# The four row-group tails of a head's scores put in front of its four wide matmuls

## The reference

```python
q, k, v = (split_heads(x @ w + b) for w, b in ((wq, bq), (wk, bk), (wv, bv)))
scores = jnp.einsum('bhqd,bhkd->bhqk', q, k) * scaling + attn_bias[:, None, :, :]
attn = jax.nn.softmax(scores, axis=-1)
ctx = jnp.einsum('bhij,bhjd->bhid', attn, v)        # then the output projection wo, bo
x = _rmsnorm(x + attn_out, alpha1, gamma1)
x = _rmsnorm(x + silu(x @ w1 + b1) @ w2 + b2, alpha2, gamma2)
return _layernorm(x_in + x)
```

## Time and profile before

| | before |
|---|---|
| median of three executions | 1919.23 us |
| the profiled execution's own time | 1920.35 us |
| its span, first to last instruction | 1918.6 us |
| mean granted TensorE clock | 0.995 |
| TensorE matmuls busy | 1888.5 us (98%) |
| VectorE busy | 1332.1 us (69%) |
| ScalarE busy | 1142.0 us (60%) |
| GpSimd busy | 1127.9 us (59%) |

### The profile page before, as it was taken

How to read it: one execution, slowest core, us unless ns; L and a number is a source line. 1 busy time by engine, 2 the same in 40 slices (tenths; PEclk the granted TensorE clock), 3 DMA queues, 4 the chain that set the end, 5 groups by cost and what they waited for, 6 DMA issues and landing times. The chain is left out here.

```text
span 1918.6 us, 39576 instructions
## 1 busy us (share of the span) xinstructions
PE 1888.5 (98%) x10336; PEld 1604.8 (84%) x10336; DVE 1332.1 (69%) x2579; ACT 1142.0 (60%) x2056; POOL 1127.9 (59%) x1739
## 2 busy tenths in 40 slices
PE   6999999999999999999999999999999999999998
PEld 5777777777777777777778999999999999999997
DVE  5777777777777777777886656656666666566754
ACT  3777777777777777777785444434444434444432
POOL 3655445554455544655687655767655667666643
PEclk8999999999999999999999999999999999999999
DMA  5555544555445554465543222112222111222101
GB/s 175 141 152 149 161 125 129 157 148 159 126 130 157 150 155 128 131 183 163 156 136 119 88 88 87 56 44 75 87 87 87 63 46 66 87 87 87 34 25 42
DMA packets 118731, 214.36 MB, mean 112 GB/s; under 512 B 19488, under 2 KB 47904, under 8 KB 116768
## 3 DMA queue, kind: packets, MB, share of 16 engines
q1 hardware_dynamic: 118688, 213.87, 36.8%
HBM read 108.93 MB, written 41.94 MB: 79 GB/s over the span
## 5 line engine op out<-in xcount | busy, mean ns | idle before, releaser
L1015 DVE TENSOR_TENSOR pT_lo<-ps_t,pT_hi 128x512 fp32r<-128x512 f32 x512 | 349.3, 688 | 98.1 <-ACT pT_hi L798 96.5
L798 ACT ACTIVATE pT_hi<-ps_t 128x512 fp32r<-128x512 f32 x512 | 303.5, 596 | 147.1 <-PE ps_t L1275 139.4
L791 ACT ACTIVATE probs<-probs,neg_max 128x512 f32<-128x512 f32 x512 | 357.2, 721 | 33.5 <-DVE neg_max L1008 32.4
L1008 DVE CUSTOM_DVE_ANT_0 probs<-ps_s,adj_s 128x512 f32<-128x512 f32 x448 | 294.7, 684 | 58.5 <-PE ps_s L1267 32.5
L1275 PE MATMUL ps_t<-ident,probs 128*128 128x128 f32 x2048 | 314.5, 278 | 7.4 <-DVE pT_lo L1015 4.8
L1275 PEld LDWEIGHTS ps_t<-ident,probs 128*128 128x128 f32 x2048 | 243.3, 141 | 92.2 <-issue 34.1
L1787 DVE TENSOR_TENSOR h_lo<-hidden,h_hi 128x512 fp32r<-128x512 f32 x192 | 170.2, 887 | 166.7 <-ACT h_hi L1694 166.6
L666 POOL CAST k_wide<-k_wide 32x512 fp32r<-32x512 f32 x128 | 78.0, 609 | 315.0 <-DMA k_wide<-weights_hi 290.5
L670 POOL CAST tails<-k_wide 16x512 fp32r<-16x512 f32 x384 | 233.3, 608 | 50.6
L1891 PE MATMUL ps_y<-w_hi,h_hi 128*128 128x384 f32 x768 | 258.2, 336 | 0.0
L1891 PE MATMUL ps_y<-w_hi,h_lo 128*128 128x384 f32 x768 | 257.1, 335 | 0.0
(11 more groups left out here) (114 smaller groups left out, 3959.6 us busy)
## 6 DMA issues: line engine op xcount, KB each, us to landing
ctx_dram<-ctx_stage SPq DMA_DIRECT2D x128, 224.0 KB
ctx_raw<-ctx_dram SPq DMA_DIRECT2D x15, 1792.0 KB, 7.3
q_wide<-weights_lo SPq DMA_DIRECT2D x192, 96.0 KB, 2.3
k_wide<-weights_hi SPq DMA_DIRECT2D x192, 96.0 KB, 2.4
adj_first<-in_adj SPq DMA_DIRECT2D x32, 512.0 KB, 6.6
adj_s<-in_adj SPq DMA_DIRECT2D x32, 512.0 KB, 6.4
rows<-in_xT SPq DMA_DIRECT2D x16, 768.0 KB, 5.0
rows<-in_x SPq DMA_DIRECT2D x16, 768.0 KB, 6.3
```

Of the source, the lines that this page charges most:

```text
L791: nc.scalar.activation(probs[:, at, :], probs[:, at, :], ACT.Exp, scale=-1.0, bias=neg_max[:, at:at + 1]).then_inc(exp_done, 1)
L798: nc.scalar.activation(pT_hi[:, h % 2, qt, :, :], ps_t[qt % 2][:, :].rearrange("p (k i) -> p k i", k=TT), ACT.Copy)\
L1008: nc.vector.tensor_tensor_reduce(out=probs[:, at, :], in0=ps_s[qt][:, :], in1=rows, scale=-1.0, scalar=BIG, op0=ALU.add, op1=ALU.min, accu ...
L1015: nc.vector.tensor_tensor(pT_lo[:, h % 2, qt, :, :].rearrange("p k i -> p (k i)"), ps_t[qt % 2][:, :], pT_hi[:, h % 2, qt, :, :].rearrange ...
```

## The change

In `scores`, the wait for the bank of `qt` 3 of the head before is taken once, in front of everything, in place of four waits, one ahead of each wide matmul. The four tails are then issued first and begin the banks; the four wide matmuls follow, end the banks, and each increments `scores_ready`. The number and the shapes of the matmuls, their operands and the count of increments are the same.

```diff
                 pe.wait_ge(tails_copied, tails_no(b, h))
-                for qt in range(TT):
-
-                    wait_past(pe, logits_ready, score_no(b, h, qt) - TT)
-                    toks = slice(qt * P, (qt + 1) * P)
-                    nc.tensor.matmul(ps_s[qt][:, :], lhsT=wide_of["q"][:, h, toks], rhs=wide_of["k"][:, h, :],
-                                     start=True, stop=False)
+                wait_past(pe, logits_ready, score_no(b, h, TT - 1) - TT)
                 for qt in range(TT):
                     if qt == OWN:
                         q_tail, k_tail = tail(tails, OWN)[:, h, qt * P:(qt + 1) * P], wide_of["k"][TAIL:DH, h, :]
                     else:
                         q_tail, k_tail = tail(q_tails, qt)[:, h, :], tail(tails, qt)[:, h, :]
-                    nc.tensor.matmul(ps_s[qt][:, :], lhsT=q_tail, rhs=k_tail,
+                    nc.tensor.matmul(ps_s[qt][:, :], lhsT=q_tail, rhs=k_tail, start=True, stop=False)
+                for qt in range(TT):
+                    toks = slice(qt * P, (qt + 1) * P)
+                    nc.tensor.matmul(ps_s[qt][:, :], lhsT=wide_of["q"][:, h, toks], rhs=wide_of["k"][:, h, :],
                                      start=False, stop=True).then_inc(scores_ready, 1)
```

## The result

| | before | after |
|---|---|---|
| median of 19 executions each | 1919.33 us | 1923.57 us |
| lowest, highest | 1918.05, 1921.33 | 1921.40, 1924.88 |
| profiled execution: own time, span | 1920.35, 1918.6 us | 1923.25, 1921.4 us |
| TensorE matmuls busy | 1888.5 us | 1890.7 us |

The ratio is 1.002, 95% interval [1.0013, 1.0026]: the change makes the kernel some 4.2 us slower, and the interval reaches from 2.5 to 5.0 us. Forecast were 5.3 us (1924.5). In the two profiled executions the difference is 2.9 us.

What follows compares the result with a forecast made beforehand. TensorE was taken as the bound, its matmuls busy 895.30 of 900 us in attention. Open heads 4.7, head 1 0.3 and head 4's wait 0.3 sum to 5.3 us: 1924.5 us, own range 1921.8 to 1926.8, whole range 1920.5 to 1928.

Steps and rivals of the forecast that it cites:

- Entering: Tails behind transposes: surcharge of 0.10 us on the stream distance, tails 0.21 after the last transpose; no difference to before.
- The cheap and the dear entry: Cheap: entry under 0.05, 1913.6 us, 7 in 100 with another case; dear: tails 0.33 after transposes, 1937.5, 4 in 100.
- Leaving: From tails into the first wide matmul: 0.11 us instead of 0.05 into transposes, so 0.05 to 0.06 more.
- open: Heads whose longer scores no wait covers: 2, 4, 5, 6, 7 and next batch's 0; 94 x 0.05 = 4.7 us.
- The cover at head 3: Transposes behind head 3's scores wait for VectorE's `pT_low(b, 2, 2)`; 0.35 us of slack covers head 3, batches 1 to 15.
- The wait: At head 4, the last bank's `logits_ready` wait ahead of the first tail: 0.02 us a batch, 0.3 us in all.
- scores of head 1: Before, a 112-column matmul followed, costing 0.09, so only 0.02 us more; 0.3 us over 15 batches.
- the rival of the earlier banks: VectorE starts logits up to 0.5 us earlier, TensorE's `pT_low` waits shrink, no change in time; 11 in 100.
- The bound of 3.2 us: TensorE's recorded waits for `pT_low`, taken as the most earlier banks could give back: 1921.3 us.

Runs made afterwards that it cites:

- The middle position: Changed kernel with the four tails between the first two and last two wide matmuls, banks 0 and 1 waited for singly: 1923.48 us, ratio 1.002.
- the run with the wait alone: Kernel before, wide matmuls still first, with the one wait for the last bank in front of everything: 1921.57 us, ratio 1.001.
- the changed kernel with the earlier `pT_low`: Changed kernel with VectorE's `pT_low(b, 2, 2)` moved ahead of `logits(b, 3, 2)`: 1923.12 us, ratio 1.0016.
- the first move alone: Kernel before with VectorE's `pT_low(b, 2, 2)` moved ahead of `logits(b, 3, 2)`: 1918.20 us, ratio 0.9992.
- both gave 4.8: Kernel before with `pT_low(b, 2, 2)` moved ahead of `logits(b, 3, 2)` and `pT_low(b, 3, 1)` ahead of `logits(b, 4, 1)`: 1914.37 us, ratio 0.9974.
- Taking 0.65 us a head: Changed kernel without the four tails of each head, so not the same result: 1899.48 us, ratio 0.9896.

## Why the prediction was right

**The sum.** Forecast 5.3 us, measured 4.2, with an interval up to 5.0. The direction and the mechanism hold; the sum is a little large.

**Entering.** Taken as 0.10 above the stream behind a transpose, from the row behind a wide matmul, with bounds of 0 and 0.22; the trace has 0.53 to the tails (forecast 0.54). The cheap and the dear entry both fall.

**Leaving.** Forecast 0.05 more a head: 0.34 from the first to the second wide matmul came as said, the whole head at 2.36 to 2.37 as said. The middle position has the loss, and the version that leaves into transposes at four heads, three of them open, has 2.5 us less of it, where 2.2 were expected. That is shown. That it is the open load of the weights is read from the load's rows (the earlier trace rows and 411.29 above); no run changed the load alone. The Trainium skill's rule that changing the tiling mode drains TensorE ("TensorEngine Tiling (Array Packing)", "Tiling Modes") agrees with all placements: no load ran ahead at a change, behind whichever neighbour.

**The cover at head 3.** Forecast as full. After the change the matmul ahead of those transposes starts at 421.64 and they at 422.16: 0.52 in place of 0.58. The 0.06 of head 3's scores came out of the wait.

**The wait.** Forecast 0.02 a batch, found 0. The two ends were reckoned to meet within 0.01, with a signal of 0.12 taken from `pT_low`. The signal of the logits is shorter: where the wait does hold TensorE back, in the run with the wait alone and in the changed kernel with the earlier `pT_low`, the next load starts 0.05 to 0.06 after their end. So the wait was over 0.04 to 0.05 before the tails could start. The run with the wait alone shows that this is the luck of the order.

**Where the sum is too large.** The distances from start to start, added up place by place in both traces over the same twelve batches (medians, us a batch):

| place | forecast | found |
|---|---|---|
| scores of heads 2, 4, 5, 6, 7 and 0 | 0.30 | 0.31 |
| scores of head 1 | 0.02 | 0.01 |
| scores of head 3, and the cover behind them | 0 | 0.06 - 0.06 |
| head 4's wait | 0.02 | 0 (within the first row) |
| a short wait behind head 0's scores | 0 | -0.04 |
| all | 0.34 | 0.26 to 0.27 |

The six open heads came as forecast. What the sum left out is the short wait behind head 0's scores, which TensorE's rows of waits do not show. In the kernel before, the last matmul ahead of the next four transposes starts at 394.33, they at 394.57, and the next matmul at 394.96; the load of the transposes stood for ScalarE's exponent. After, the exponent is there in time:

```profile
394.54 0.42 PEld L1275 LDWEIGHTS ps_t<-ident,probs 128*128 128x128 f32 x4 [0.25 <-ACT probs L791]
394.57 0.63 PE L1275 MATMUL ps_t<-ident,probs 128*128 128x128 f32 x4
...
394.96 0.47 PE L1288 MATMUL ps_g<-pT_hi,v_s 128*112 128x512 f32 x1
```
```profile
395.24 0.60 PE L1273 MATMUL ps_t<-ident,probs 128*128 128x128 f32 x4
395.60 0.48 PE L1286 MATMUL ps_g<-pT_hi,v_s 128*112 128x512 f32 x1
```

From the transposes to the next matmul it is 0.39 before and 0.36 after, and the 0.01 ahead of them goes too. This is the rival of the earlier banks, true for 0.04 us a batch, some 0.6 us in all. It is read from the two traces; the middle position, with its equally early banks, has the 0.36 as well, and no run changed the banks' time alone. The bound of 3.2 us that the prediction gave this rival was no bound: that row of waits undercounts, as the place at head 3 alone holds TensorE for 0.35 us a batch, 5 us in all. The rival failed as a whole because that place gave back only the 0.06 by which head 3's scores grew; the prediction had said that the work it waits for begins at a projection and not at scores.

By the batch, 15 x 0.26 is 3.9 us, and the medians differ by 4.2. The 2.9 us between the two profiled executions are how single executions lie to their medians (1.0 above before, 0.3 below after).

## What to carry to other kernels

A block of row-group matmuls paid twice here, entering and leaving, and the second price depended on what stood behind it: put the instruction with the cheapest weight load there, here a transpose, not a 128-column float32r matmul. Ask of a wait that is moved forward what covers it now, and what it takes from the next improvement; the same wait cost 2 us in one order and nothing in another. A row of short waits is no measure of standing time: compare distances from start to start with those of a plain stream. Where a queue is 99% busy, look for the one instruction of another engine that is late in every batch, and after moving it, for the next: the first move alone gave 1.4 us, not quite clear of the noise, both gave 4.8.

## What was not expected of the hardware

Taking 0.65 us a head from the engine that is busy for 98% of the time gave 24 of 70 us: on the far side of this kernel's balance stand a transfer, with about half of the missing time, and many short waits. And the 0.05 us that each head's scores grew by was paid nearly in full: 0.37 us a batch with head 3, of which 0.10 came back. Close to balance the two directions have different prices.
